# Third layer's gate weights by repeating transfers instead of a matmul, the shared expert first in each batch

## Chip, cores and metric

One core of a Trainium2 chip. The metric is device time in microseconds (us) of one execution of the whole kernel. Lower is better.

## What is computed

The reference is a stack of four layers on x of shape (4, 512, 128) in float32. Each layer has an attention-like block and a feed-forward block, each behind a layer norm and a gate tanh(g). The change touches the feed-forward block of the third layer (`L2_...` in the reference, `l == 2` in the kernel), a mixture of 32 small experts and one shared expert:

```
scores = sigmoid(X @ gate_w.T)
idx = top_k(scores + bias, 4)
w = scores[idx] / sum(scores[idx])
valid = position of the row in its expert's queue < 128
h_e = silu(X @ W1[e]) * (X @ W3[e])        # 64 hidden numbers for each of 32 experts
out = sum over the chosen, valid e of  w_e * (h_e @ W2[e])
out = out + (silu(X @ sw1.T) * (X @ sw3.T)) @ sw2.T
```

The kernel computes all 32 experts for all rows and multiplies the hidden numbers by the weight w_e, which is zero where a row did not choose the expert.

## The kernel before

The kernel is one program with hand-written instruction streams for five sequencers: `sync` (SP, issues transfers), `gpsimd` (POOL), `scalar` (ACT), `tensor` (PE) and `vector` (DVE). They meet at semaphores only (`wait_ge`, `then_inc`), and each engine takes its instructions in the written order, so a wait holds all that is written behind it.

**Units.** In the third layer's feed-forward block the work is cut into 4 batches of 512 rows (`b`) and 17 units in each (`c`). A routed unit holds a pair of experts, 2 x 64 hidden numbers on 128 partitions, for 512 rows; there are 16 (`ROUTED[2]`). The unit c = 16 is the shared expert. A unit goes through five steps:

1. `gu` on PE: two products for the gate (bank G) and two for the up projection (bank U), from the two parts `xt_hi` and `xt_lo` of the transposed input. For a routed unit a fifth matmul, called the pick here, multiplies the 0/1 matrix `pair_sel` by `comb_t`, the weights of all 32 experts turned and split into three bf16 parts. It spreads the two weight rows of this unit over 2 x 64 partitions of bank W.
2. `unit` on ACT: silu of G into the ring `hb` of four buffers (L887). `high` on ACT: copy of the bank W to one of three buffers `wsb` (L900).
3. `mult` on DVE: hb times U (L2303).
4. `low` on POOL: hb times wsb (L672); not for the shared expert.
5. `down` on PE: `wa_hi` times hb, summed over the 17 units in the bank ACC.

PE runs `gu` three units ahead of `down` (`AHEAD = 3`): at step c of the loop it does `gu` of unit c + 3, then `down` of unit c, then what else is written at this step. All matmuls go through a helper and carry L1172; the tile names tell them apart (`xt_hi,wa_hi`, `comb_t,pair_sel` the pick, `hb,wa_hi` the down).

**What lies between the units.** During batch b the next batch is prepared: layer norm (`moments`, `scale_rows`), transposition, logits on PE (`PE_LOGITS` = 5), the choice of experts in seven parts on DVE at the steps of `ROUTE_AT[2]`, the running count of rows in each expert on PE (`running`, step `PE_RUN` = 11), its use in `route_end` on DVE (`WEIGH_AT[2]` = 14), the turned weights on PE (`comb_in`, step `PE_COMB[2]` = 13) and their copy on ACT (`pre_comb`, `COMBT_AT[2]` = 16). In batches 0 and 1 the Fourier filter of the third layer's other block runs for batches 2 and 3 at the steps of `fft_steps`: moments, `split_halves` on DVE, `transform` on PE, `filter_products` on DVE, `inverse` on PE, `fft_update` on DVE. From unit 20 on, `chain` also puts the fourth layer's attention and routing in between. All of these share the one bank T: each use waits until the one before is read (`T_free`).

**Transfers.** SP issues transfers in one written order: the last of them before the fourth layer are `rows_of(2)` and `rows_of(3)` (L537, results of the second layer), and after `x_done` of the last Fourier update the fourth layer's weights (L589 to L592: three transfers of 16 experts' matrices, three of the shared expert's).

Of the kernel before, what the change touches and what calls it, by code (L numbers as in the profile page):

```python
# [14 lines left out]
F32 = mybir.dt.float32  # L15
# [8 lines left out]
TB = S // 128  # L24
# [188 lines left out]
def build(nc, a, out, s1, s3, y3, stages=8):  # L213
    with ExitStack() as ctx:
# [6 lines left out]
        def sem(name):  # L221
# [86 lines left out]
        d_x = [sem(f"d_x{b}") for b in range(B)]  # L308
        d_stage = [sem(f"d_stage{i}") for i in range(2)]
# [5 lines left out]
            um_done wcopy_done w_used zp_set ids_set sel3_done cum3_ps idx3_done cnt3_ps nb3_done incl3_ps  # L315
# [73 lines left out]
        wsb = nc.alloc_sbuf_tensor_at("wsb", [128, 3, 512], F32, offset=at["h_hi"])  # L389
        wpr = nc.alloc_sbuf_tensor_at("wpr", [128, E1, 4, 128], F32, offset=at["wa_lo"])[:, :, :, :]  # L390
# [33 lines left out]
        def slots(layer, c):  # L424

            if layer == 0:
                return (c, 16 + c, 32 + c) if c < 16 else (48, 49, 50)
            if layer == 2:
                return (c, 16 + c, 32 + c) if c < 16 else (48, 49, 50)
            return c, 20 + c, 40 + c  # L430
# [55 lines left out]
        ROUTE_AT = [(8, 9, 10, 11, 12, 13, 13), (16, 16, 16, 17, 18, 19, 20), (8, 8, 8, 9, 10, 11, 12), (8, 8, 8, 9, 10, 11, 12)]  # L486
        COUNT_AT = 10
        WEIGH_AT = [14, 21, 14, 13]
        COMBT_AT = [16, 24, 16, 15]
        PE_BACK, PE_XN, PE_LOGITS, PE_RUN = 0, 2, 5, 11  # L490
        PE_COMB = [13, 21, 13, 12]
# [4 lines left out]
        def fft_steps(l, b):  # L496


            if l == 2 and b < 2:
                return 2 + b, (4, 7, 8, 11, 10, 13)  # L500
# [5 lines left out]
        def _(sp):  # L506
# [80 lines left out]
            sp.wait_ge(q["x_done"], x_num(4, 3))  # L587
            for i, w in enumerate(("routed_w1", "routed_w2", "routed_w3")):
                sp.dma_start(pk3[:, :, F3 * i:F3 * i + F3], a["L3_ffn_" + w].rearrange("e d h -> d e h")).then_inc(d_wl, 16)  # L589
            sp.dma_start(hi_flat[:, 0:512], a["L3_ffn_shared_w1"][0]).then_inc(d_wl, 16)  # L590
            sp.dma_start(hi_flat[:, 512:1024], a["L3_ffn_shared_w2"][0]).then_inc(d_wl, 16)
            sp.dma_start(sw3, a["L3_ffn_shared_w3"][0].rearrange("(c h) d -> h c d", c=4)).then_inc(d_wl, 16)  # L592
# [29 lines left out]
        def _(pool):  # L622
# [1982 lines left out]
```

## Time and profile before

| what | value |
|---|---|
| median of 3 runs | 880.02 us (879.59 to 883.28) |
| the profiled execution | 879.37 us, of it the span of the profile 877.6 us |
| mean granted TensorE clock | 0.934 of full speed |
| PE busy in the span | 754.7 us (86%) |
| DVE, ACT, POOL busy | 560.9, 375.4, 390.2 us |
| third layer's feed-forward block | about 538 to 731 us of the span |

Busy PE time is modelled: a matmul is shown from its start to its end, and the next starts before that. The distance from start to start is the better price of one in a row of many.

### The profile page before, as it was taken

How to read it: one execution, taken by the hardware profiler on the slowest of the kernel's cores; microseconds unless marked ns; L12 is line 12 of the kernel's file. 1: busy time of each engine (PE TensorE's matmuls, PEld its weight loads, DVE VectorE, ACT ScalarE, POOL GpSimd, SP SyncE). 2: the span in 40 equal slices, each digit the busy share in tenths (PEclk: the TensorE clock that was granted, in tenths of full speed). 3: DMA queues.
4: the chain of work that ended last, by engine and by line, in shares of the span. 5: the costliest groups of instructions: out<-in, count | busy, mean ns of one | idle time of the engine just before them, and what ended most of it. 6: DMA issues, size and time to landing. Idle time of an engine off the chain costs nothing.

```text
span 877.6 us, 14107 instructions
## 1 busy us (share of the span) xinstructions
PE 754.7 (86%) x3936; PEld 536.6 (61%) x3936; DVE 560.9 (64%) x1813; ACT 375.4 (43%) x834; POOL 390.2 (44%) x381
## 2 busy tenths in 40 slices
PE   6999789999999878875997887999989887988885
PEld 3577656666767545665887885565555553645553
DVE  3377778878788278863533766978767644524554
ACT  0244244444445335524554434456455564213331
POOL 2000034545455435372764434555455663345661
PEclk8899989999999879955999998999999999899998
DMA  5023999800000311015677642000600000022325
GB/s 144 13 61 110 337 332 333 260 1 1 0 1 1 89 20 31 18 38 177 190 213 213 188 116 55 1 1 1 174 13 10 10 13 13 17 59 80 88 53 144
DMA packets 74396, 79.36 MB, mean 90 GB/s; under 512 B 17769, under 2 KB 61424, under 8 KB 74194
## 3 DMA queue, kind: packets, MB, share of 16 engines
q1 hardware_dynamic: 68112, 69.49, 27.4%
q0 software_dynamic: 5024, 8.54, 2.9%
q8 instruction: 35, 0.57, 0.3%
q10 hardware_dynamic: 1186, 0.43, 0.2%
q14 instruction: 39, 0.32, 0.1%
HBM read 40.48 MB, written 39.85 MB: 92 GB/s over the span
## 4 chain that ended last, share of the span: by engine, by line
PE 57%; DVE 23%; issue 7%; ACT 4%; POOL 3%; DMA 3%; SPq 1%; ACTq 0%; POOLq 0%; DVEq 0%
PE psum L1172 52%; DVE hb L2305 2%; DVE hb L2306 1%; POOL s L740 1%; DVE hb L2303 1%; DVE mr L1970 1%; DVE const L1926 1%; PE psum L1231 1%; POOL s L718 1%; PE psum L1621 1%; PE psum L1691 1%; DMA chosen<-in_mask_1x1xSxS_ik 1%; DVE l_lo L1886 1%; DVE wk L1927 1%; DMA l_hi<-y 1%
## 5 line engine op out<-in xcount | busy, mean ns | idle before, releaser
L677 POOL TENSOR_TENSOR h_lo<-hb,h_hi 128x512 fp32r<-128x512 f32 x68 | 87.8, 1294 | 119.7 <-ACT h_hi L905 119.6
L1172 PE MATMUL psum<-xt_hi,wa_hi 128*128 128x512 f32 x272 | 129.0, 474 | 13.1 <-DVE hb L2306 8.4
L745 POOL DMA_INDIRECT y<-xn x93 | 92.3, 993 | 77.7 <-DVE xn L2062 37.2
L887 ACT ACTIVATE hb<-psum 128x512 f32<-128x512 f32 x136 | 81.0, 595 | 81.5 <-PE psum L1172 81.3
L1172 PE MATMUL psum<-xt_lo,wa_hi 128*128 128x512 f32 x272 | 108.4, 399 | 0.0
L672 POOL TENSOR_TENSOR hb<-hb,wsb 128x512 f32<-128x512 f32 x64 | 82.1, 1283 | 56.2 <-DVE hb L2303 49.3
L1172 PEld LDWEIGHTS psum<-xt_hi,wa_hi 128*128 128x128 f32 x272 | 52.7, 194 | 36.0 <-DVE hb L2306 14.1
L2303 DVE TENSOR_TENSOR hb<-hb,psum 128x512 f32<-128x512 f32 x68 | 46.0, 684 | 39.9 <-ACT hb L887 29.4
L1172 PE MATMUL psum<-hb,wa_hi 128*128 128x512 f32 x136 | 70.9, 602 | 0.5 <-POOLq L674 0.5
L1172 PE MATMUL psum<-l_lo,l_hi 128*128 (+1 forms) x204 | 57.1, 380 | 10.9 <-issue 5.6
L1172 PEld LDWEIGHTS psum<-xt_lo,wa_hi 128*128 128x128 f32 x272 | 52.5, 193 | 16.1 <-issue 7.5
L648 POOL TENSOR_TENSOR rstd<-veps,neghalf 128x4 f32<-128x4 f32 x20 | 20.3, 1016 | 92.9 <-DVE veps L1864 92.1
L905 ACT ACTIVATE h_hi<-hb 128x512 fp32r<-128x512 f32 x68 | 42.7, 627 | 42.0 <-DVE hb L2306 41.4
L2305 DVE TENSOR_TENSOR hb<-hb,psum 128x512 f32<-128x512 f32 x64 | 43.7, 683 | 22.5 <-PE psum L1172 17.3
L1172 PE MATMUL psum<-comb_t,pair_sel 96*128 96x512 bf16 x128 | 50.8, 397 | 5.7 <-ACT wsb L900 5.0
L1172 PE MATMUL psum<-xt_hi,wa_lo 128*128 128x512 f32 x136 | 53.6, 394 | 0.0
L1172 PE MATMUL psum<-wpr,hb 128*128 x368 | 49.4, 278 | 0.3 <-issue 0.3
L1172 PEld LDWEIGHTS psum<-l_lo,l_hi 128*128 128x128 f32 x204 | 31.6, 192 | 27.5 <-issue 24.2
L1172 PEld LDWEIGHTS psum<-wpr,hb 128*128 128x128 f32 x368 | 45.8, 196 | 0.5 <-issue 0.5
L2306 DVE TENSOR_TENSOR hb<-hb,psum 128x512 f32<-128x512 f32 x64 | 44.0, 687 | 2.2
L718 POOL DMA_INDIRECT s<-l_hi,l_lo x32 | 31.3, 978 | 26.8 <-DVE l_hi L2200 14.5
L740 POOL DMA_INDIRECT s<-l_hi,l_lo x32 | 31.7, 992 | 25.4 <-DVE l_hi L2200 9.0
(353 smaller groups left out, 1714.6 us busy)
## 6 DMA issues: line engine op xcount, KB each, us to landing
s<-l_lo SPq DMA_DIRECT2D x20, 1386.0 KB, 16.8
l_hi<-in_pack SPq DMA_DIRECT2D x24, 322.0 KB, 3.3
l_lo<-in_pack SPq DMA_DIRECT2D x22, 322.0 KB, 3.7
xn<-s SPq DMA_DIRECT2D x93, 66.0 KB
stage<-in_pack SPq DMA_DIRECT2D x13, 256.0 KB, 2.6
y_in<-y SPq DMA_DIRECT2D x8, 256.0 KB, 4.0
l_hi<-y SPq DMA_DIRECT2D x8, 256.0 KB, 5.0
stage<-in_L_ffn_W SPq DMA_DIRECT2D x12, 128.0 KB, 2.3
```

What stands on the lines that cost most here:

```text
L648: pool.tensor_tensor(rstd[:, :], veps[:, :], neghalf[:, :], ALU.pow).then_inc(q["rstd_set"], 1)
L672: pool.tensor_tensor(hb[:, k % 4, :], hb[:, k % 4, :], wsb[:, w % 3, :], ALU.mult).then_inc(q["w_used"], 1)
L677: pool.tensor_tensor(h_lo[:, k % 3, :], hb[:, k % 4, :], h_hi[:, k % 3, :].bitcast(F32), ALU.subtract).then_inc(q["hlo_pool"], 1)
L718: pool.indirect_dma_start(s1, bass.IndirectOffsetOnAxis(idx3[:, n, i, k:k + 1], 0), xs3[i][:, TB * n + k, :], None).then_inc(d_scat1[n // ...
L740: pool.indirect_dma_start(s3, bass.IndirectOffsetOnAxis(idx3[:, n, i, k:k + 1], 0), xs3[i][:, TB * n + k, :], None).then_inc(d_scat, 16)
L745: pool.indirect_dma_start(y3, bass.IndirectOffsetOnAxis(xe3[:, j % XE, 128:129].bitcast(I32), 0), xe3[:, j % XE, 0:128], None, bounds_chec ...
L887: act.activation(hb[:, k % 4, :], G[k % 2][:, :], ACT.Silu).then_inc(q["sg_done"], 1)
L905: act.activation(h_hi[:, k % 3, :], hb[:, k % 4, :], ACT.Copy).then_inc(q["hhi_done"], 1)
L1172: return pe.matmul(o, l, r, start=start, stop=stop, skip_group_check=True)
L2303: dve.tensor_tensor(h, h, U[k % 2][:, :], ALU.mult).then_inc(q["um_done"], 1)
L2305: link(dve.tensor_tensor(h, h, U[k % 2][:, :], ALU.mult))
L2306: dve.tensor_tensor(h, h, W[k % 2][:, :], ALU.mult).then_inc(q["h_done"], 1)
```

## The change

- `comb_in` of the third layer turns the float32 weights (`wfin`, four transposes) instead of three bf16 parts. `route_end` on DVE ends with the multiplication that writes `wfin`; the four instructions that split it fall away for this layer.
- `pre_comb` on ACT copies the turned weights (32 x 512) to `wt2` and issues a transfer of them to a new table `wd` in device memory (4 x 32 x 512 float32).
- SP then loads, for each of the 64 routed units, two rows of `wd`, each repeated over 64 partitions, into one of the three buffers `wsb` (two transfers of 64 x 2 KB). It waits for the table of the batch, and from the fourth load on for POOL to be done with the buffer.
- The pick on PE and the copy `high` on ACT fall away for this layer. POOL's `low` waits for the transfer instead of the copy.
- The shared expert is unit c = 0 of each batch; the routed pairs are c = 1 to 16.
- The fourth layer's weights are loaded from within this sequence, behind the load for routed unit 36 (the fifth of batch 2), as `load_layer3()`.
- Steps move: route parts from (8, 8, 8, 9, 10, 11, 12) to (8, 8, 8, 8, 9, 9, 10), `PE_RUN` 11 to 8, `WEIGH_AT` 14 to 11, `PE_COMB` 13 to 10, `COMBT_AT` 16 to 13, the Fourier steps from (4, 7, 8, 11, 10, 13) to (6, 9, 12, 14, 14, 16).

```diff
+        d_wt, WT0 = d_wnat, 16 * 4
+        d_wb, WB0 = d_w1[0:3], [16 * len(range(i, NB1, WS)) for i in range(3)]
...
+        wt2 = nc.alloc_sbuf_tensor_at("wt2", [32, 512], F32, offset=at["comb_t"])
+        wfin = nc.alloc_sbuf_tensor_at("wfin", [128, TB, 32], F32, offset=at["chl"])
...
+            for b in range(B):
+                for c in range(ROUTED[2]):
+                    w = b * ROUTED[2] + c
+                    if c == 0:
+                        sp.wait_ge(d_wt, WT0 + 16 * (b + 1))
+                    if w >= 3:
+                        sp.wait_ge(q["w_used"], w - 2)
+                    for e in range(2):
+                        sp.dma_start(wsb[64 * e:64 * e + 64, w % 3, :],
+                                     wd[b, 2 * c + e:2 * c + e + 1, :].broadcast_to([64, S])).then_inc(d_wb[w % 3], 16)
+                    if w == 2 * ROUTED[2] + 4:
+                        load_layer3()
...
-                    if c >= ROUTED[2]:
+                    if c == 0:
                         pool.sem_inc(q["h_done"], 1)
                         return
-                    w = b * ROUTED[2] + c
-                    pool.wait_ge(q["wcopy_done"], w + 1)
+                    w = b * ROUTED[2] + c - 1
+                    pool.wait_ge(d_wb[w % 3], WB0[w % 3] + 32 * (w // 3 + 1))
...
+                if l == 2:
+                    if b:
+                        act.wait_ge(d_wt, WT0 + 16 * b)
+                    act.activation(wt2[:, :], T[0:32, :], ACT.Copy).then_inc(q["combt_done"], 1)
+                    act.wait_ge(q["combt_done"], fnum(l, b))
+                    act.dma_start(wd[b], wt2[:, :]).then_inc(d_wt, 16)
+                    return
...
-                    act.wait_ge(q["u_done"], UB[2] + k - CB[2] + 1)
-                    if w >= 3:
-                        act.wait_ge(q["w_used"], w - 2)
-                    if w == 0:
-                        act.wait_ge(q["down_done"], CB[2])
-                    act.activation(wsb[:, w % 3, :], W[0][:, :], ACT.Copy).then_inc(q["wcopy_done"], 1)
...
-                if l == 2 and k - CB[2] >= 1:
-                    pe.wait_ge(q["wcopy_done"], sum(1 for i in range(k - CB[2]) if i % NC[2] < ROUTED[2]))
...
-                    last = mm(W[0 if l == 2 else k % 2][:, :], pick, comb_t[0:3 * N_EXP[l], b % 2, :], True, True)
+                    last = mm(W[k % 2][:, :], pick, comb_t[0:3 * N_EXP[l], b % 2, :], True, True)
...
-                    link(dve.tensor_tensor(w_, w_, m_, ALU.mult))
+                    dve.tensor_tensor(wfin[:, :, :], w_, m_, ALU.mult).then_inc(q["comb_done"], 1)
+                    return
```

## Rows read from the trace of the kernel before

**Rows 1.** The page: the chain that ended last, by engine.

```profile
PE 57%; DVE 23%; issue 7%; ACT 4%; POOL 3%; DMA 3%; SPq 1%; ACTq 0%; POOLq 0%; DVEq 0%
```

**Rows 2.** Stretches: length, then PE, PEld, DVE, ACT, POOL busy, PEclk, DMA, GB/s.

```profile
545.00:580.00 35.00, 34.02 (x153) 20.99 (x152) 32.54 (x79) 17.13 (x31) 19.64 (x16) 1.00 0.00 1
...
590.00:618.00 28.00, 26.94 (x129) 17.16 (x128) 24.54 (x75) 16.54 (x30) 13.61 (x12) 1.00 0.00 1
```

**Rows 3.** The chain that ended last, by line, 545 to 727 us.

```profile
by line: PE psum L1172 56.9%; issue 6.8%; DVE hb L2303 5.5%; DVE wk L1909 2.1%; ACT hb L887 2.0%; ACT L887 1.8%; DVE mr L1970 1.5%; ACT wsb L900 1.5%; PE psum L1249 1.4%; DVE ch L2086 1.4%; DVE l_lo L1886 1.4%; DVE l_lo L2190 1.3%; DVE wk L
```

**Rows 4.** Timeline around a routed unit: start us, us, engine, line, operation.

```profile
562.14 0.39 PE L1172 MATMUL psum<-comb_t,pair_sel 96*128 96x512 bf16 x1
...
562.37 1.02 PE L1172 MATMUL psum<-hb,wa_hi 128*128 128x512 f32 x2
...
562.68 0.69 DVE L2303 TENSOR_TENSOR hb<-hb,psum 128x512 f32<-128x512 f32 x1
...
563.45 1.28 POOL L672 TENSOR_TENSOR hb<-hb,wsb 128x512 f32<-128x512 f32 x1 [0.95 <-DVE hb L2303]
...
564.15 0.39 PE L1172 MATMUL psum<-comb_t,pair_sel 96*128 96x512 bf16 x1
```

**Rows 5.** PE's waits, 545 to 727 us: us in total, times, longest.

```profile
PE psum L1172 <- ACT wsb L900: 5.0, 11, 0.7
...
PE psum L1172 <- DVEq L2347: 1.1, 1, 1.1
```

**Rows 6.** Timeline of the block's start.

```profile
536.49 0.29 DVE L2167 TENSOR_TENSOR chosen<-chosen 128x128 f32<-128x128 f32 x1
...
538.01 0.66 PE L1409 MATMUL psum<-ident_bf,chl 128*96 128x128 bf16 x4 [3.40 <-DVE chl L2171]
...
539.30 2.03 SPq L537 DMA_DIRECT2D y_in<-y  x4
...
545.40 1.02 PE L1172 MATMUL psum<-hb,wa_hi 128*128 128x512 f32 x2
```

**Rows 7.** Two stretches of that start, columns as in Rows 2.

```profile
538.00:540.00 2.00, 1.99 (x8) 1.56 (x8) 0.00 (x0) 1.27 (x2) 0.00 (x0) 0.50 0.01 0
...
544.00:545.00 1.00, 1.00 (x6) 0.77 (x5) 0.47 (x1) 0.90 (x3) 1.00 (x2) 1.00 0.38 107
```

**Rows 8.** Timeline of SP's queue: the fourth layer's weights, first and last issue.

```profile
621.89 6.25 SPq L589 DMA_DIRECT2D l_lo<-in_L_ffn_routed_w  x3
...
632.22 0.43 SPq L592 DMA_DIRECT2D l_hi<-in_L_ffn_shared_w  x1
```

**Rows 9.** Line 592, the last of these transfers: issue to landing.

```profile
DMA to landing us min/median/max: 5.7/5.7/5.7
```

**Rows 10.** DMA issues: KB each, median us from issue to landing.

```profile
y_in<-y SPq DMA_DIRECT2D x8, 256.0 KB, 4.0
...
stage<-in_L_ffn_W SPq DMA_DIRECT2D x12, 128.0 KB, 2.3
```

**Rows 11.** A stretch of the fourth layer's loading, columns as in Rows 2.

```profile
626.00:628.00 2.00, 1.90 (x11) 1.06 (x10) 0.66 (x1) 1.76 (x4) 1.28 (x1) 1.00 1.07 295
```

**Rows 12.** Timeline, batch 2: POOL at c = 2 and c = 6, PE's down of c = 6.

```profile
637.62 1.28 POOL L672 TENSOR_TENSOR hb<-hb,wsb 128x512 f32<-128x512 f32 x1 [1.48 <-DVE hb L2303]
...
651.71 1.29 POOL L672 TENSOR_TENSOR hb<-hb,wsb 128x512 f32<-128x512 f32 x1
...
656.22 1.02 PE L1172 MATMUL psum<-hb,wa_hi 128*128 128x512 f32 x2
```

**Rows 13.** Timeline of DVE in batch 0: scaling for the filter, and routing scores.

```profile
556.55 3.19 DVE L1872 TENSOR_SCALAR wk<-x,mv,rstd 128x128 f32<-128x128 f32 x4
...
561.31 1.34 DVE L2086 TENSOR_TENSOR ch<-rt,small 128x128 f32<-128x128 f32 x1
```

**Rows 14.** Timeline of the block's last units: PE's down, POOL's multiplication.

```profile
725.42 1.12 PE L1172 MATMUL psum<-hb,wa_hi 128*128 128x512 f32 x2 [0.48 <-POOLq L674]
...
725.58 1.27 POOL L672 TENSOR_TENSOR hb<-hb,wsb 128x512 f32<-128x512 f32 x1 [0.27 <-POOL hb L672]
```

More of the change, by code:

```diff
@@ L210, in link, with build @@
         self.eng.wait_ge(self.sem, self.n)
-def build(nc, a, out, s1, s3, y3, stages=8):
+def build(nc, a, out, s1, s3, y3, wd, stages=8):
     with ExitStack() as ctx:
@@ L427, in slots @@
                 return (c, 16 + c, 32 + c) if c < 16 else (48, 49, 50)
-            if layer == 2:
-                return (c, 16 + c, 32 + c) if c < 16 else (48, 49, 50)
-            return c, 20 + c, 40 + c
+            return (c - 1, 15 + c, 31 + c) if c else (48, 49, 50)
         block = ctx.enter_context(nc.Block())
@@ L484, in build @@
         NORM_AT, OUT_AT, XN_AT, ADD_AT, XHI_AT, XLO_AT, SCORE_AT = 0, 2, 3, 3, 5, 6, 8
-        ROUTE_AT = [(8, 9, 10, 11, 12, 13, 13), (16, 16, 16, 17, 18, 19, 20), (8, 8, 8, 9, 10, 11, 12), (8, 8, 8, 9, 10, 11, 12)]
+        ROUTE_AT = [(8, 9, 10, 11, 12, 13, 13), (16, 16, 16, 17, 18, 19, 20), (8, 8, 8, 8, 9, 9, 10), (8, 8, 8, 9, 10, 11, 12)]
         COUNT_AT = 10
[L488 to L491, printed above, removed]
+        WEIGH_AT = [14, 21, 11, 13]
+        COMBT_AT = [16, 24, 13, 15]
+        PE_BACK, PE_XN, PE_LOGITS, PE_RUN = 0, 2, 5, 8
+        PE_COMB = [13, 21, 10, 12]
         NORM2_AT, XN2_AT = 4, 7
@@ L586, in _, with load_layer3 @@
             rows_of(3)
[L587 to L592, printed above, removed]
+            def load_layer3():
+                sp.wait_ge(q["x_done"], x_num(4, 3))
+                for i, w in enumerate(("routed_w1", "routed_w2", "routed_w3")):
+                    sp.dma_start(pk3[:, :, F3 * i:F3 * i + F3], a["L3_ffn_" + w].rearrange("e d h -> d e h")).then_inc(d_wl, 16)
+                sp.dma_start(hi_flat[:, 0:512], a["L3_ffn_shared_w1"][0]).then_inc(d_wl, 16)
+                sp.dma_start(hi_flat[:, 512:1024], a["L3_ffn_shared_w2"][0]).then_inc(d_wl, 16)
+                sp.dma_start(sw3, a["L3_ffn_shared_w3"][0].rearrange("(c h) d -> h c d", c=4)).then_inc(d_wl, 16)
+            for b in range(B):
[10 more added lines that the diff above has]
+                        load_layer3()
             sp.wait_ge(q["tabi_done"], 3)
@@ L1139, in _ @@
                             k = b * NC[l] + c
-                            if l == 2:
-                                high(l, b, c)
-                            elif k >= 1:
+                            if l != 2 and k >= 1:
                                 pb, pc = divmod(k - 1, NC[l])
@@ L1407, in comb_in @@
                 use_t()
-                for k in range(TB):
+                for k in range(TB if l == 2 else 0):
+                    last = pe.transpose(T[0:32, 128 * k:128 * k + 128], wfin[:, k, :], ident)
+                for k in range(0 if l == 2 else TB):
                     last = pe.transpose(T[:, :].bitcast(BF16)[0:rows, 128 * k:128 * k + 128], chl[:, k, 0:rows], ident_bf[:, :])
@@ L1435, in gu @@
                 last = product(U[k % 2][:, :], us)
-                if l == 2 and k - CB[2] >= 1:
-                    pe.wait_ge(q["wcopy_done"], sum(1 for i in range(k - CB[2]) if i % NC[2] < ROUTED[2]))
-                if c == 0:
+                if l == 0 and c == 0:
                     pe.wait_ge(q["combt_done"], fnum(l, b))
-                if c < ROUTED[l]:
-                    if N_EXP[l] == 32:
-                        pick = pair_sel[:, 2 * c:2 * c + 2, :].rearrange("p e i -> p (e i)")
-                    else:
-                        pick = sel16[:, c:c + 1].broadcast_to([48, 128])
-                    last = mm(W[0 if l == 2 else k % 2][:, :], pick, comb_t[0:3 * N_EXP[l], b % 2, :], True, True)
+                if l == 0 and c < ROUTED[l]:
+                    pick = pair_sel[:, 2 * c:2 * c + 2, :].rearrange("p e i -> p (e i)")
+                    last = mm(W[k % 2][:, :], pick, comb_t[0:3 * N_EXP[l], b % 2, :], True, True)
                 last.then_inc(q["u_done"], 1)
@@ L2601 @@
     y3 = nc.dram_tensor("y3", (2 * B * S, D), F32, kind="Internal").ap()
-    build(nc, a, out, s1, s3, y3, STAGES)
+    wd = nc.dram_tensor("wd", (B, 32, S), F32, kind="Internal").ap()
+    build(nc, a, out, s1, s3, y3, wd, STAGES)
     r = run_bass_kernel_spmd(nc, [arrays], core_ids=[0])
```

9 lines of the change are left out of this document (2 added, 7 removed).

## The prediction

> **What bounds the kernel now.** I read the page's chain first: of the whole span PE holds 57% of the chain that ended last, DVE 23% [rows 1]. Then the same chain over the block that the change touches: PE's matmuls 56.9%, the rest split over many DVE and ACT lines, and 1.5% for the ACT copy that the change removes [rows 3]. So PE sets the pace for something under two thirds of the block, and for the rest PE stands or would soon stand behind DVE. The busy time by stretch says where: from 545 to 580 us PE is busy 34.0 and DVE 32.5 of 35 us, from 590 to 618 us 26.9 and 24.5 of 28 [rows 2]. PE has hardly a gap, but DVE is close behind it; what PE saves there soon meets DVE. Last, the timeline of one unit: two picks in neighbouring units start at 562.14 and 564.15, so a routed unit costs PE 2.01 us, and the pick takes 562.14 to 562.37 of it, 0.23 us [rows 4].
>
> **What the picks give.** There are 64 picks. Four or five of them lie in the start (below); 59 x 0.23 = 13.6 us of PE time are left. All of it comes off the time only if PE is the path throughout. I take 0.6 of it, the share of the chain over the block that is PE's (56.9% and a little for other PE lines [rows 3]): 8.1 us. Ends: 5 us if DVE closes up early, 13.6 us if not at all.
>
> **What the ACT copies give.** PE waited 11 times, 5.0 us in all, for the copy to free the bank W [rows 5]; that wait is gone. The copy's share of the chain is 1.5% of 182 us = 2.7 us [rows 3]. I take 2.7; ends 0 and 5.0. The copies' other time on ACT was beside other work.
>
> **What DVE saves.** From the multiplication at 536.49 to the start of PE's transposes at 538.01 lie 1.52 us, of them about 0.35 for the multiplication; the split costs 1.15 us [rows 6]. Once per batch: the first belongs to the start. Of the other three, 3.4 us, a third is on the path: 1.0 us; ends 0 and 3.4. The four transposes in float32 instead of bf16 I cost at nothing; there are three such places outside the start, and even at twice their 0.66 us [rows 6] they would be under 2 us, a third of it on the path.
>
> **The start.** PE waited 3.4 us for the weights, started at 538.01 and reached its first down at 545.40 [rows 6]. Without the split it starts 1.15 us earlier. Its clock is granted at half (1.2 GHz) at 538 to 540 and is full (2.4 GHz) at 544 to 545 [rows 7]; at the half clock a pick costs twice 0.23, so the first five picks are worth some 1.7 us. But now a chain of transfers stands before POOL's first multiplication. SP issues four transfers of `rows_of` until 541.33 [rows 6], which run until 544.4 (0.38 of the last microsecond [rows 7]); the rows for the first routed unit are written behind them. The table itself is ready before: transposes and copy end near 538.2, and a small transfer takes 2.3 us [rows 10]. The first rows therefore land near 544.4 + 0.4 + 1.0 = 545.8, POOL ends at 547.1 [its 1.28 in rows 4], and PE's down of c = 1 starts at 547.2. Before it stood at 545.40 + 2.02 = 547.4. Of 2.9 us saved 0.2 to 0.4 arrive: I take 0.4. Ends: 2.9, and a loss of 2.
>
> **One unit's transfers, steady.** Two issues of about 0.4 us (as line 592 [rows 8]), then 2.3 us for 128 KB [rows 10] and about 0.4 us for the second 128 KB at the 295 GB/s of the fourth layer's loading [rows 11]: 3.5 us. Three buffers go round in 3.5 + 1.3 (POOL) + 0.2 = 5.0 us, 1.7 us a unit, below the 2.01 - 0.23 = 1.78 us that PE needs. So they are hidden, narrowly; at the mean pace of the block, (727 - 545) / 68 = 2.7 us before and some 2.6 after, amply. Since (6.3 + 1.5) / 3 = 2.6, up to 6.3 us for a pair costs nothing on average. The nearest rows for the other end are the 256 KB with 4.0 us [rows 10], so up to 5.5 us. At a batch's first unit the table is ready in time: PE turns it at step 10, eight units (20 us) before its first row is multiplied.
>
> **The fourth layer's weights.** This is the queue that matters. Before, nobody waited for them. Now rows are written before and behind them in SP's order. SP issues them from 621.89 to 632.65 [rows 8], and the last lands at 632.22 + 5.7 = 637.9 [rows 8, 9]: 16.0 us, with the transfer engines full [rows 11]. SP reaches them when POOL is done with routed unit 33, which is c = 2 of batch 2. The rows of unit 37 (c = 6) can land only 0.9 (the issue of unit 36) + 16.0 + 1.4 (its own data and that of unit 36) = 18.3 us after that. Before, POOL ended c = 2 at 638.90 and began c = 6 at 651.71, 12.8 us [rows 12]; with a faster PE some 12. POOL stands 6.3 us. PE is less hit: its down of c = 6 began at 656.22, 3.2 us after POOL's end at 653.00 [rows 12]. So PE stands 3.1 us, and falls to half clock for a time, as after the wait of 3.4 us [rows 6, 7]; at half clock for about 3 us it loses 1.4 more. I take +4.5 us; ends 0 (DVE is late there anyway, and works ahead meanwhile) and 11 (no slack, and a load that is stretched by the rows between).
>
> Here the Trainium skill has a rule, in DMA: Bandwidth & Descriptors, section Queues, rings and completion order: each transfer engine takes the descriptors of one issuing engine's ring in order. By it the rows of unit 37 wait for the whole load. Rows 8 and 9 agree as far as they go, with the last issued landing 16 us after the first issue. If the order did not hold, this term would be near 0 and the sum 4.5 us lower.
>
> **The last unit.** Before, the shared expert closed the block, and needed no POOL. Now the last down waits for POOL's 1.27 us behind the unit before it [rows 14]: +1.4 us; ends 1 and 2.
>
> **The moved steps.** Before, `running` stood at step 11 of PE behind the Fourier update of DVE's step 13 in bank T; PE waited 1.1 us for that once [rows 5]. That goes: -1.1. But DVE's step 9 now holds marking, choice and, in batches 0 and 1, the scaling for the filter (3.19 us) and the split; its step 8 the scores (1.34 us) [rows 13] and the top values. Together the steps 8 and 9 have some 10 us of DVE work against 2 units of PE (4 us), and PE's `comb_in` at step 10 waits for DVE's step 11. A lead of up to three units pays most of it. I take +1.5 us for the two batches; ends 0 and 5.
>
> **Sum.** -8.1 - 2.7 - 1.0 - 0.4 + 4.5 + 1.4 - 1.1 + 1.5 = -5.9 us. The profiled execution took 879.37, so 873.5; the median stands 0.65 higher, so 874.
>
> **Rivals.**
>
> *DVE closes up (no change).* For it: DVE at 93% from 545 to 580 us [rows 2]. The picks then give 5 us, the copies 1, and the terms of cost stay: -5 - 1 - 1 - 0.4 + 4.5 + 1.4 - 1.1 + 2.5 = 0: 880. Against it: from 618 us on DVE has gaps. The change would then do what it says, off the path.
>
> *PE's whole saving arrives.* -13.6 - 5.0 - 2 - 0.4 + 2 + 1.4 - 1.1 + 0 = -18.7: 861. It needs DVE to keep ahead everywhere; against it the near-equal loads of rows 2.
>
> *The fourth layer's load is worse (within or above).* The term at its end of 11, the rest as forecast: 880.5.
>
> *Repeated rows are read slowly (slower).* All 64 copies of a row come from the same 2 KB of memory, which no row of the trace shows. It decides from 6.3 us for a pair on; POOL waits in each unit. At 7 us a unit takes (7 + 1.5) / 3 = 2.83 us instead of 2.6, over 64 units +15 us on the forecast: 889. At 8 us it is +36: 910. Against it: rates of 295 GB/s for 512-byte pieces from separate places [rows 11], and 2 KB pieces here. The Trainium skill, same page, section Latency and other measured facts, tells of loads whose rows lie a large power of two apart and run at half rate (103 of 207 GB/s), with reads falling on the same part of memory as its guess. By it the 256 KB of a pair would take 2.5 us instead of 0.9 and the pair 5.1, still under the point from which it decides; no row here shows it.
>
> **Chances.** Forecast (867 to 876): 0.42. PE's whole saving (below 867): 0.10. DVE closes up: 0.20. Load worse: 0.12. Slow rows: 0.16. Faster by over 0.5% (below 875.6; 0.5% is about what this measurement can tell from no change): 0.50. Within: 0.26. Slower (above 884.4): 0.24. The range 862 to 888 leaves out half of the second case and the worse half of the last one; the forecast's own range is 867 to 876.
>
> **What would show it.** Right: the block some 6 us shorter; one stand of POOL of about 6 us at routed unit 37 with transfer engines full, and PE at half clock behind it; no PE wait for a copy; the first POOL multiplication near 545.8; the last down behind POOL. The landing of a pair at 3 to 4 us shows the rate; 7 or more, with POOL idle before each unit, shows the slow rows. A longer PE wait before the turned weights of batches 1 and 2 shows DVE's crowded step 9. I am wrong if PE's matmuls keep their spacing of 2.0 us because DVE holds them, or if the stand at unit 37 is absent or beyond 10 us.

## The result and the profile after

| | before | after |
|---|---|---|
| median of 4 runs | 879.81 us (878.27 to 883.28) | 896.46 us (894.50 to 897.05) |
| span of the profiled execution | 877.6 us | 894.4 us |
| mean granted clock | 0.934 | 0.916 |
| PE, DVE, ACT, POOL busy | 754.7, 560.9, 375.4, 390.2 us | 754.8, 543.6, 340.4, 390.1 us |

The ratio is 1.0178 [1.0151, 1.0205]: the change makes the kernel 1.8% slower, some 16 us, where I had forecast 0.7% faster. (Before was run again beside each set of experiments, with medians from 879.8 to 882.7 us; a ratio compares within its set and leaves disturbed executions out. A difference of two medians carries up to 3 us of that drift, so where both are given the ratio is the better figure. Where a ratio is turned into us below, it is taken times 881 us.)

The page's groups first, to see that the change does what it says. Columns: line, engine, tiles, shape, count, busy us, mean ns, then idle time before and what ended most of it; then the issues with KB each and us to landing.

```profile
L690 POOL TENSOR_TENSOR hb<-hb,wsb 128x512 f32<-128x512 f32 x64 | 82.1, 1282 | 55.4 <-DVE hb L2313 37.1
...
L2313 DVE TENSOR_TENSOR hb<-hb,psum 128x512 f32<-128x512 f32 x68 | 45.7, 684 | 36.7 <-ACT hb L912 31.1
...
wsb<-wd SPq DMA_DIRECT2D x128, 128.0 KB, 2.8
```

There are 128 row loads, no pick and no copy, and ACT lost 35 us of work. A transfer of repeated rows lands in 2.8 us, so a pair with its two issues of 0.6 takes 3.4 to 4.0 us, near the 3.5 assumed. Yet PE is busy as long as before over the span: 13.6 us of picks are gone, and the other matmuls took that much longer in sum. In the block itself (from the turned weights to the last batch's end) PE is busy 173.2 us instead of 177.0, and idle 32.0 us instead of 15.5. The reason is in the waits, and the clock behind them. PE's waits, 536 to 760 us (us in total, times, longest):

```profile
PE psum L1184 <- POOLq L692: 12.1, 3, 7.4
PE psum L1184 <- DVE hb L2313: 11.4, 11, 2.0
PE psum L1280 <- DVE wk L1918: 7.2, 3, 5.3
PE psum L1421 <- DVE wfin L2176: 2.2, 1, 2.2
```

The same before, 536 to 731 us, besides [rows 5]:

```profile
PE psum L1172 <- DVE hb L2303: 4.2, 4, 1.8
PE psum L1268 <- DVE wk L1909: 3.7, 3, 1.6
PE psum L1172 <- POOLq L674: 0.5, 1, 0.5
```

Line 1184 is PE's matmul helper, 692 POOL's hand-over of a routed unit, 1280 the transposition of the fourth layer's attention probabilities, 1421 `comb_in`. The 5.0 us of waiting for ACT's copies [rows 5] are gone; in their place are 12.1 us for POOL where there were 0.5, and 18.6 us for DVE (lines 2313 and 1918) where there were 7.9. The longest sit at three places.

**The fourth layer's weights, batch 2.** SP's queue, then POOL and PE (start us, us, engine, line; idle before in brackets):

```profile
651.83 7.86 SPq L594 DMA_DIRECT2D l_lo<-in_L_ffn_routed_w  x3
659.74 3.31 SPq L595 DMA_DIRECT2D l_hi<-in_L_ffn_shared_w  x1
663.10 0.43 SPq L596 DMA_DIRECT2D l_hi<-in_L_ffn_shared_w  x1
663.57 0.46 SPq L597 DMA_DIRECT2D l_hi<-in_L_ffn_shared_w  x1
664.08 4.45 SPq L607 DMA_DIRECT2D wsb<-wd  x6
```

```profile
659.82 1.28 POOL L690 TENSOR_TENSOR hb<-hb,wsb 128x512 f32<-128x512 f32 x1 [2.13 <-DVE hb L2313]
662.01 1.06 POOL L758 DMA_INDIRECT s<-l_hi,l_lo  x1 [0.91 <-POOL hb L690]
671.48 1.25 POOL L690 TENSOR_TENSOR hb<-hb,wsb 128x512 f32<-128x512 f32 x1 [8.41 <-issue]
```

```profile
665.04 0.40 PE L1184 MATMUL psum<-xt_lo,wa_hi 128*128 128x512 f32 x1
672.84 2.08 PE L1184 MATMUL psum<-hb,wa_hi 128*128 128x512 f32 x2 [7.40 <-POOLq L692]
```

Stretches around it (length; PE, PEld, DVE, ACT, POOL busy; clock, DMA share, GB/s):

```profile
660.00:668.00 8.00, 5.44 (x26) 3.63 (x25) 3.26 (x12) 3.13 (x5) 2.16 (x2) 1.00 1.03 297
668.00:670.00 2.00, 0.00 (x0) 0.00 (x0) 0.00 (x0) 0.00 (x0) 0.00 (x0) 0.89 0.96 220
670.00:682.00 12.00, 9.16 (x21) 5.83 (x22) 4.03 (x17) 2.25 (x4) 6.79 (x6) 0.50 0.27 88
```

From the first issue to POOL's multiplication of routed unit 37 lie 19.6 us; I had forecast 17.4. The timeline says "issue" where POOL waits for this transfer; the transfer engines at 1.03 and 0.96 show what it was. PE stands 7.4 us, until 672.84. The clock falls to half, 1.2 GHz, during the stand, between 669 and 670 us, and all that PE does from 672.84 to 682 it does at half: the down that takes 1.02 us [rows 12] takes 2.08. Of these 9.16 us of matmuls half would have sufficed, so the clock costs another 4.6 us. Here the Trainium skill's rule (DMA: Bandwidth & Descriptors, section Queues, rings and completion order: descriptors of one ring are taken in order) agrees with the trace: the load's last piece, issued at 663.57, landed 7.1 us later, at 670.7, and the six row transfers behind it took 4.5 to 6.7 us to land instead of 2.8. But that is the smaller part. SP needed from 651.83 to 664.08, 12.2 us, to issue the load, and before that it could not issue a row at all.

**Batch 1, the routing and the fourth layer's attention.** DVE, then PE:

```profile
615.21 0.75 DVE L2142 TENSOR_SCALAR chosen<-mr 128x128 f32<-128x128 f32 x1
...
616.46 1.12 DVE L1881 TENSOR_SCALAR wk<-x,mv,rstd 128x128 f32<-128x128 f32 x4
617.61 0.42 DVE L2324 TENSOR_TENSOR wk<-wk 128x256 f32<-128x256 f32 x1
...
619.20 1.13 DVE L2160 TENSOR_SCALAR wsum<-wsum 128x4 f32<-128x4 f32 x1
...
621.43 0.29 DVE L1918 TENSOR_TENSOR wk<-wk,const 128x128 f32<-128x128 f32 x1
```

```profile
621.78 1.03 PE L1280 MATMUL psum<-const,wk 128*32 128x128 f32 x4 [5.25 <-DVE wk L1918]
```

Marking, Fourier scale, split and weights all stand ahead of the normalisation of the attention (L1918), for which PE waits 5.25 us. Before, the same wait in this batch was 0.6 us.

**The start.** PE, then POOL:

```profile
542.47 0.61 PE L1421 MATMUL psum<-const,wfin 128*32 128x128 f32 x4 [2.23 <-DVE wfin L2176]
...
549.39 1.02 PE L1184 MATMUL psum<-hb,wa_hi 128*128 128x512 f32 x2
...
554.15 2.07 PE L1184 MATMUL psum<-hb,wa_hi 128*128 128x512 f32 x2 [2.81 <-POOLq L692]
```

```profile
552.58 1.46 POOL L690 TENSOR_TENSOR hb<-hb,wsb 128x512 f32<-128x512 f32 x1 [3.28 <-DMA wsb<-wd]
```

The first multiplication comes 10.1 us after the turned weights; PE stands 2.8 us, and its matmuls take twice as long, at a granted clock of 0.50 from 554 to 560 us. From the turned weights to the down of c = 1 pass 11.7 us (542.47 to 554.15); before, 9.4 (538.01 to 547.42).

**Where in the block.** From each trace I take the start of the turned weights' transposes and the four starts of the `out_back` transposes (each at step 0 of the next batch, the last at the block's end), and get four stretches that can be compared. Behind the label stands the ratio to before of all its runs. The last column is the time in the block at the half clock: twice the sum of (1 - PEclk) times length over stretches of about 5 us:

| kernel | ratio | block begins | batch 0 | 1 | 2 | 3 | block | at half clock |
|---|---|---|---|---|---|---|---|---|
| before | | 538.0 | 50.0 | 50.1 | 51.1 | 41.3 | 192.5 | 9 |
| after | 1.0178 | 542.5 | 54.9 | 51.1 | 57.2 | 42.1 | 205.3 | 34 |
| l3_spread | 1.0070 | 538.2 | 55.3 | 51.0 | 49.1 | 40.9 | 196.3 | 18 |
| old_steps | 1.0033 | 537.6 | 49.6 | 47.6 | 56.2 | 42.1 | 195.6 | 25 |
| spread_old | 0.9994 | 540.4 | 49.9 | 47.6 | 48.2 | 40.6 | 186.2 | 12 |
| dummy_picks | 1.0060 | 543.8 | 51.0 | 49.3 | 50.0 | 44.2 | 194.7 | 12 |
| picks_shared_first | 1.0003 | 542.5 | 49.9 | 49.0 | 48.7 | 43.2 | 190.8 | 4 |
| picks_new_order | 1.0136 | 545.9 | 54.2 | 55.2 | 51.1 | 42.6 | 203.1 | 13 |
| fft_wide | 1.0020 | 540.0 | 52.9 | 50.7 | 48.3 | 42.3 | 194.2 | 24 |
| transform_late | 1.0050 | 539.5 | 53.0 | 52.0 | 50.2 | 41.6 | 196.7 | 26 |

The block begins anywhere from 534.9 to 546.6 us in the 20 traces of this study, 541.3 on average in the four kernels' traces with picks and the old copies and 540.6 in the sixteen without, so the 4.5 us by which it begins later here are hardly the change's. The scatter goes with the clock ahead of the block: 78 us at the half clock where the block begins earliest, 90 in before, 113 where it begins latest. The 12.8 us in the block are the change's; the ratio says 15.7 (13.3 to 18.1), and the traces don't place the difference. A block's length scatters too: in the traces of spread_old, first_rows_early and few_rows_old (all below), with the same routing and Fourier steps, it is 186.2, 191.5 and 191.9 us.

### The profile page after: what moved, and what is told of

Its sections match the earlier page's. It is cut to its first block, busy times and chain, and to the rows that moved or that the text cites. A ratio compares the mean times of both kernels' runs of the same rounds, so it can differ in the third digit from the quotient of the medians.

```text
span 894.4 us, 13966 instructions
## 1 busy us (share of the span) xinstructions
PE 754.8 (84%) x3872; PEld 543.9 (61%) x3872; DVE 543.6 (61%) x1797; ACT 340.4 (38%) x770; POOL 390.1 (44%) x381
## 4 chain that ended last, share of the span: by engine, by line
PE 56%; DVE 23%; issue 8%; POOL 4%; DMA 3%; ACT 3%; SPq 1%; ACTq 0%; POOLq 0%; DVEq 0%
PE psum L1184 51%; DVE hb L2315 2%; DVE hb L2313 2%; DVE hb L2316 1%; POOL s L758 1%; DVE mr L1979 1%; PE psum L1243 1%; DVE const L1935 1%; POOL s L736 1%; PE psum L1630 1%; PE psum L1700 1%; DMA chosen<-in_mask_1x1xSxS_ik 1%; DVE wk L1936 1%; DMA l_hi<-y 1%; POOL hb L690 1%
## 5 line engine op out<-in xcount | busy, mean ns | idle before, releaser
L1184 PE MATMUL psum<-xt_hi,wa_hi 128*128 128x512 f32 x272 | 131.7, 484 | 20.2 <-DVE hb L2313 11.4
L1184 PE MATMUL psum<-hb,wa_hi 128*128 128x512 f32 x136 | 76.0, 642 | 12.1 <-POOLq L692 12.1
L1184 PE MATMUL psum<-l_lo,l_hi 128*128 (+1 forms) x204 | 57.3, 380 | 10.8 <-issue 5.6
L919 ACT ACTIVATE h_hi<-hb 128x512 fp32r<-128x512 f32 x68 | 42.6, 627 | 41.9 <-DVE hb L2316 41.4
L1184 PE MATMUL psum<-wpr,hb 128*128 x368 | 49.9, 280 | 0.3 <-issue 0.3
L986 ACT ACTIVATE hb<-psum,l_hi 128x128 f32<-128x128 f32 x96 | 27.4, 368 | 32.0 <-PE psum L1184 32.0
```

The source lines that it names most:

```text
L919: act.activation(h_hi[:, k % 3, :], hb[:, k % 4, :], ACT.Copy).then_inc(q["hhi_done"], 1)
L986: last = act.activation(hb[:, j % 4, 128 * c:128 * c + 128], G[j % 2][:, 128 * c:128 * c + 128], ACT.Gelu_apprx_tanh, bias=w1s[j % WS][:, ...
L1184: return pe.matmul(o, l, r, start=start, stop=stop, skip_group_check=True)
```

## The experiments

**l3_spread: the load in small pieces.**

```diff
-                    if w == 2 * ROUTED[2] + 4:
-                        load_layer3()
+                    if 0 <= w - (2 * ROUTED[2] + 4) < 15:
+                        load_layer3(w - (2 * ROUTED[2] + 4))
...
+                if j < 12:
+                    i, g = divmod(j, 4)
+                    w = ("routed_w1", "routed_w2", "routed_w3")[i]
+                    sp.dma_start(pk3[:, 4 * g:4 * g + 4, F3 * i:F3 * i + F3],
+                                 a["L3_ffn_" + w][4 * g:4 * g + 4].rearrange("e d h -> d e h")).then_inc(d_wl, 16)
```

> The changed kernel, but the fourth layer's weights in 15 transfers of 256 KB, one behind each of the row loads 36 to 50, instead of all behind load 36. Theory A (the stand of PE at routed unit 37, 7.4 us in the trace of the changed kernel, and the half clock behind it until 683 us cost 11 to 13 us): 883 to 886 us, no PE wait over 2 us in batch 2, clock full there. Rival B (the stand only uses time that DVE would have taken anyway, or the row loads slow PE's loop everywhere): under 4 us gained, 892 to 897.

888.77 us, ratio 1.0070 [1.0037, 1.0104]. The stand of 7.4 us is gone and batch 2 falls from 57.2 to 49.1 us. The load in one piece cost 7.7 us by the medians, 9.5 by the ratios, less than theory A and more than rival B.

**old_steps: the steps of before, the rest as changed.**

```diff
-        WEIGH_AT = [14, 21, 11, 13]
-        COMBT_AT = [16, 24, 13, 15]
-        PE_BACK, PE_XN, PE_LOGITS, PE_RUN = 0, 2, 5, 8
-        PE_COMB = [13, 21, 10, 12]
+        WEIGH_AT = [14, 21, 14, 13]
+        COMBT_AT = [16, 24, 16, 15]
+        PE_BACK, PE_XN, PE_LOGITS, PE_RUN = 0, 2, 5, 11
+        PE_COMB = [13, 21, 13, 12]
...
-                return 2 + b, (6, 9, 12, 14, 14, 16)
+                return 2 + b, (4, 7, 8, 11, 10, 13)
```

> The changed kernel with the steps of before: route parts, running count, turned weights and Fourier steps at their old places; rows by transfer and shared expert first stay. Theory A (DVE's crowded step 9 of batch 1 holds the fourth layer's attention and so PE for 5.3 us, plus some 2 us of half clock): 6 to 8 us faster than the changed kernel, 888 to 891, and no wait of that size before the turned probabilities. Rival C (the moved steps are neutral, what is won at one place is lost at another, such as the old coupling of the running count to the Fourier update): within 2 us of 896.5.

886.84 us, ratio 1.0033 [0.9995, 1.0071]: 9.6 us by the medians, 12.8 by the ratios, more than even theory A. Batches 0 and 1 fall by 5.3 and 3.5 us. This was the bigger surprise: I had priced these steps at 1.5 - 1.1 = +0.4 us.

**picks_new_order: before, with the shared expert first and the new steps; picks and copies stay.**

```diff
+            return (c - 1, 15 + c, 31 + c) if c else (48, 49, 50)
...
-                return 2 + b, (4, 7, 8, 11, 10, 13)
+                return 2 + b, (6, 9, 12, 14, 14, 16)
```

> The kernel before (picks on PE, copies on ACT), but the shared expert first in each batch and the moved steps of the change. Theory A (the moved steps cost 6 to 8 us, the last routed unit 1.5): 887 to 890. Rival C (order and steps are neutral; all the loss is in the transfers): 880 to 882.

894.38 us, ratio 1.0136 [1.0104, 1.0169]. Without a single row load, order and steps cost 12 us, again above both forecasts.

**before_again: the kernel before, unchanged.**

> The kernel before, unchanged, profiled once more. In the changed kernel the block started 4.5 us later than in the first profile of before, though nothing ahead of it was changed. If that is chance from run to run, this profile lies anywhere from 538 to 543 us at the first turned weights; if it belongs to the changed program, this one is again at 538 us.

880.41 us. Its block took 192.5 us, as in the first trace, and batches 0 and 1 50.1 each. It begins at 538.9 us, with 89 us at the half clock ahead of it. That looked like the program's own beginning; the other traces with picks, at 542.5 and 545.9, say that it is not.

**spread_old: l3_spread and old_steps together.**

> The changed kernel with both repairs: the fourth layer's weights in fifteen transfers of 256 KB, one behind each of the row loads 36 to 50, and the steps of the kernel before. Theory (two separate costs, the load and the crowded steps): the two savings of 7.7 and 9.6 us add, 896.5 - 17.3 = 879, about equal to before or a little faster, with no PE wait of more than 4 us for POOL. Rival (the same time is saved twice, because the DVE that stands behind is the bound after either repair): 884 to 887. Rival (faster than both kernels, since the picks and copies are gone): 872 to 876.

881.73 us, ratio 0.9994 [0.9966, 1.0021]. Both savings are there; together they give back the whole 1.8%, though not their sum (9.5 + 12.8). In its trace the block is 6.3 us shorter than before, begins 2.4 us later, and is followed by 149.5 us to the end of the span instead of 147.1; behind the block 23 us are at the half clock, 17 before. The whole is 1.5 us shorter in this trace, and level with before over all executions.

**picks_shared_first: before with the shared expert first, old steps.**

> The kernel before, with its picks and copies and its steps, but the shared expert first in each batch. Theory (the moved steps cost the time, the order almost nothing): 880 to 882. Rival (the order itself costs: POOL stands once per batch and works one unit later at the end, and PE's last down waits for it): 884 to 890, most of the 12 us of picks_new_order.

882.43 us, ratio 1.0003 [0.9968, 1.0039]. The order costs nothing. So the 12 us of picks_new_order are the steps'.

**few_rows: after, with 61 of 64 pairs never loaded** (POOL multiplies by old rows).

```diff
-                    for e in range(2):
+                    for e in range(2 if w < 3 else 0):
```

> The changed kernel, but only the first three pairs of rows are loaded, and POOL multiplies by those old buffers from then on; the loads of the other 61 routed units are left out, all steps and the load of the fourth layer's weights stay. Theory (the rows cost only where they queue behind the fourth layer's weights): 888 to 890, as l3_spread, and no wait of POOL for a transfer behind the first unit. Rival (the 8 MB of row loads slow other things too, ports or memory): 880 or less. Rival (the rows cost nothing, PE would stand anyway): 895.

889.46 us, ratio 1.0086 [1.0052, 1.0119], as l3_spread. The row loads (128 of 128 KB, so 16 MB and not the 8 that I had written) cost what they wait behind the fourth layer's weights, and nothing more that can be seen (1.0086 against l3_spread's 1.0070).

**few_rows_old: the same on spread_old.**

> spread_old, but only the first three pairs of rows are loaded and POOL multiplies by those old buffers from then on; the loads of the other 61 routed units are left out. It is the change with its transfers free of cost. Theory (PE's saved time is given back at DVE, not at the transfers): 880 to 882, as spread_old. Rival (the row loads still cost POOL or PE some us): 875 to 877.

882.19 us, ratio 0.9971 [0.9929, 1.0013], not to be told from spread_old (881.73 us, 0.9994). By the medians the transfers are free; the two intervals together leave anything from 6 us of cost to 2 us of gain open.

**dummy_picks: the picks put back, unread, on spread_old.**

```diff
+                if l == 2 and c:
+                    last = mm(W[0][:, :], pair_sel[:, 0:2, :].rearrange("p e i -> p (e i)"), hi.bitcast(BF16)[0:96, 0:512], True, True)
```

> spread_old with a matmul of the pick's shape (96x128 weights, 96x512 bf16 moving) put back for each of the 64 routed units, its result never read; everything else as spread_old. It prices the picks alone. Theory (PE's picks lie in time in which PE would wait for DVE, or in which the filled engine keeps its clock): 881 to 883, no change against spread_old. Rival (the picks are worth my 8 us and something else in the change costs as much): 889 to 891.

885.01 us, ratio 1.0060 [1.0037, 1.0084], 3.3 us over spread_old by the medians, 5.8 by the ratios, 8.5 in the blocks of the two traces. It lies between the two theories. The picks are worth something, 3 to 8 us, near my 8.1 at best. And with them in place the rest of the change costs 5.3 us (3.3 to 7.4), which I had forecast at a small gain.

**first_rows_early: three pairs of rows ahead of the second layer's results.**

```diff
-            rows_of(2)
-            rows_of(3)
...
+                    if w == 2:
+                        rows_of(2)
+                        rows_of(3)
...
-                            if l == 2 and b == 0 and c in (2, 3):
-                                combine1(c)
+                            if l == 2 and b == 0 and c in (4, 5):
+                                combine1(c - 2)
```

> spread_old with the loads of the first three pairs of rows ahead of the two loads of the second layer's results, whose adding on DVE moves from steps 2 and 3 to 4 and 5 of batch 0. Theory (the first multiplication on POOL waits behind those 1 MB loads, and PE falls to half clock for it): the first POOL multiplication comes 3 to 4 us earlier, 878 to 879 against 881.7. Rival (DVE holds batch 0 anyway): 881 to 882.

877.90 us, ratio 0.9974 [0.9951, 0.9997]. POOL's first multiplication:

```profile
541.71 1.26 POOL L698 TENSOR_TENSOR hb<-hb,wsb 128x512 f32<-128x512 f32 x1
```

That is 6.8 us after the turned weights (534.88) instead of 10.1 to 10.9, and batch 0 takes 48.5 us instead of 49.9. The gain over spread_old, 1.8 us by the ratios, is within both intervals.

**fft_old and route_old: half of the moved steps each.** fft_old is after with only the Fourier steps old; route_old is after with only the routing's.

> The changed kernel with only the Fourier steps of the kernel before (4, 7, 8, 11, 10, 13); routing stays at its new steps. Theory (DVE's step 9 is crowded because the Fourier scale and split were put beside the routing marks): PE's waits for the attention's probabilities shrink and most of the 9.6 us of old_steps comes back, 888 to 890. Rival (the early running count and turned weights at PE's steps 8 and 10 are what holds PE): no gain, 895 to 897. Rival (the shared bank T is taken in a worse order when only one half moves): slower than 897.

> The changed kernel with only the routing steps of the kernel before (parts, running count, weights, turned weights, copy); the Fourier steps stay at the new ones. The other half, the old Fourier steps alone, gave 899.7 us. Theory (the routing parts packed into DVE's steps 8 to 11 are the whole cost of the moved steps): 886 to 888, as with both moved back. Rival (both halves must move together, since all share the bank T): 893 or more.

fft_old 899.7 us, 1.0212 [1.0179, 1.0246]; route_old 891.66 us, 1.0105 [1.0059, 1.0150]. Neither half gives back what both do (1.0033): the old routing steps alone bring 6.4 us, between my two forecasts, and the old Fourier steps alone bring nothing. By its time fft_old is what the third possibility said, slower than 897, but its interval overlaps that of the changed kernel (1.0178 [1.0151, 1.0205]), so that it is worse is not shown. The two sets depend on each other; the runs don't show by which wait.

**parts_early: only the seven routing parts on DVE early, on spread_old.**

> spread_old with only the seven routing parts on DVE at their new steps (8, 8, 8, 8, 9, 9, 10); running count, weights, turned weights, copy and Fourier steps stay old. Theory (the parts packed together hold DVE's multiplications of two or three units, and PE stands for them): 2 to 5 us over spread_old, 884 to 887. Rival (the parts are only handed over in another order, the cost is that running count and turned weights take the bank T and PE's time early): 881 to 883.

882.17 us, ratio 1.0021 [0.9990, 1.0053]. Packing the parts is no cost that the runs can show, though its trace has batch 1 at 51.0 us with a wait of 3.8 us for the attention's normalisation (1.8 in spread_old). A cost of up to 2 us stays possible.

**new_steps_b2: the new routing steps in batch 2 alone, which has no Fourier filter.**

> spread_old with all new routing steps (parts, running count 8, weights 11, turned weights 10, copy 13), but in batch 2 only, which has no Fourier filter beside it. Theory of the prediction's term (the cost comes where the Fourier scale and split stand beside the routing, batches 0 and 1): 881 to 882. Rival (the routing's own packing costs in each batch): a third of the 12 us, 885 to 886.

877.76 us, ratio 0.9962 [0.9930, 0.9994], below both forecasts. No cost there. What the routing's steps cost, they cost in batches 0 and 1, beside the Fourier filter.

**fft_wide and transform_late: the distance between PE and DVE.** In l3_spread DVE, for once, waits for PE (DVE, then PE, batch 0):

```profile
580.87 0.42 DVE L2342 TENSOR_TENSOR wk<-l_lo,psum 128x256 f32<-128x256 f32 x1 [3.05 <-PE psum L1191]
...
587.33 0.88 DVE L2359 SCALAR_TENSOR_TENSOR x<-psum,tg,x 128x256 f32<-128x256 f32 x2 [2.88 <-PE psum L1191]
```

```profile
578.83 1.95 PE L1191 MATMUL psum<-wk,const 128*128 128x128 f32 x16
...
585.35 1.95 PE L1191 MATMUL psum<-wk,const 128*128 128x128 f32 x16
```

These are the Fourier filter's products behind `transform`, and its update behind `inverse`. Before, they stood three steps behind PE's (8 to 11, 10 to 13), with the change two (12 to 14, 14 to 16). PE runs `gu` three units ahead, so in step c of DVE, three steps on from PE's step c - 3, the products of `gu` are there already. A result that PE makes in step c - 2 may not be, and then DVE waits for it. First the edit of l3_spread to fft_wide, then that of spread_old to transform_late:

```diff
-                return 2 + b, (6, 9, 12, 14, 14, 16)
+                return 2 + b, (6, 9, 11, 14, 13, 16)
...
-                return 2 + b, (4, 7, 8, 11, 10, 13)
+                return 2 + b, (4, 7, 9, 11, 10, 13)
```

> l3_spread (all new steps) with the Fourier steps (6, 9, 11, 14, 13, 16) instead of (6, 9, 12, 14, 14, 16): PE transforms and inverts one step earlier, so that DVE's products and update stand three steps behind, as in the kernel before. Theory (DVE is held by PE because it comes two steps behind): its two waits of 3 us per batch go, the first two batches take 51 and 48 us, and the time falls from 888 to 882 to 884. Rival (the routing packed into DVE's steps 8 to 11 is the cause, the Fourier distance is not): 887 to 890.

> spread_old (all old steps) with PE's transform at step 9 instead of 8, so that DVE's products stand two steps behind it. Theory (the distance of two steps costs DVE's lead): DVE waits some 2 to 3 us for PE ahead of the products, and the time rises by 2 to 4 us over spread_old, 884 to 886. Rival (no cost by itself): 881 to 883.

fft_wide 883.38 us, 1.0020 [0.9990, 1.0051], 4.4 us under l3_spread by the ratios. transform_late 886.77 us, 1.0050 [1.0023, 1.0078], 4.9 us over spread_old. DVE's waits for PE in l3_spread, in fft_wide, in spread_old and in transform_late, 538 to 650 us:

```profile
DVE x L2359 <- PE psum L1191: 6.2, 2, 3.3
DVE wk L2342 <- PE psum L1191: 6.1, 2, 3.1
```

```profile
DVE x L2359 <- PE psum L1191: 2.6, 2, 1.7
DVE wk L2342 <- PE psum L1191: 2.5, 2, 1.3
```

```profile
DVE wk L2342 <- PE psum L1191: 1.7, 2, 1.3
```

```profile
DVE wk L2342 <- PE psum L1191: 6.2, 2, 3.5
```

One step of distance, given or taken, moves the waits by 4 to 7 us and the time by 4 to 5 (each plus or minus 3 to 4), both ways. Moving the step also moves PE's use of the bank T; no run tells that apart from the distance, though DVE's waits are for the result itself. The forecast for fft_wide was right in the time and half right in the stretches: batch 0 fell only from 55.3 to 52.9, batch 1 hardly (PE's wait for the attention stays, 5.2 us).

**shared_last: first_rows_early, with the shared expert last in batches 1 to 3.**

> first_rows_early with the shared expert first in batch 0 only and last in batches 1 to 3. Theory (with the shared expert first PE's last down waits for POOL's last multiplication, 1.4 us): 1 to 2 us under first_rows_early, 876 to 877. Rival (the end is hidden by other work): equal, 878.

880.01 us, ratio 0.9987 [0.9964, 1.0010]. No gain, where I had forecast 1 to 2 us: a last down that needs no POOL is worth nothing that can be measured.

**all_repairs: shared_last with new_steps_b2's steps.**

> The best of all: the change with the fourth layer's weights spread over fifteen loads, the steps of the kernel before in batches 0 and 1 and the new routing steps in batch 2, the first three pairs of rows ahead of the second layer's results, the shared expert first in batch 0 and last in the others. Theory (the repairs add, and the picks are worth what I forecast): 874 to 878, under before by 0.4 to 0.9%. Rival (what is won in this block is lost to what follows): 880 to 882.

880.57 us, ratio 0.9991 [0.9966, 1.0015]. A miss. The small gains of first_rows_early and new_steps_b2 don't add up; nothing here beats the kernel before by more than their 0.3 to 0.4%, of which the intervals just exclude zero.

## Why the prediction was wrong

**What the moved steps cost** is the step of the prediction that failed most: +1.5 for "crowded DVE step 9" and -1.1 for the freed bank T, together +0.4 us. Measured: 11.7 us (picks_new_order against picks_shared_first), 12.8 (after against old_steps), 6.7 where the load no longer stands in the way (l3_spread against spread_old). I had looked for what DVE does in a step, and named the right place for one part of it: the marks, the Fourier scale and the split in one run of DVE. But I let `comb_in` wait for it, and paid it from a lead of three units. In the trace the one that waits is the fourth layer's attention, queued on DVE behind all this; what that wait costs by itself stays open, for parts_early has 3.8 us of it and no slower time. And the lead itself had been cut: two steps between `transform` and the products, and between `inverse` and the update, where before there were three. The numbers (8 to 11, 12 to 14) stood in the diff. fft_wide and transform_late show that this is 4 to 5 us; of the rest the stretches tell only that it lies almost all in batches 0 and 1, and the halves that it depends on both sets of steps. Which wait carries it stays open. The -1.1 came true: the wait for bank T is in no line of the trace after.

**The fourth layer's load** was the right place at half its size: +4.5 forecast, 7.7 to 9.5 measured (the ratios leave 6 to 13). From its first issue to POOL's multiplication passed 19.6 us where I had 17.4 (18.3 less the 0.9 of issue before it). POOL was to stand 6.3 and stood 10.4 (661.10 to 671.48, with one indirect transfer of 1.06 in it): SP reached the load 9.3 us before POOL ended the last unit that had its rows, against 11 assumed. PE was 3 us less late than POOL, as I had it, hence 7.4 instead of 3.1. And PE's work at the half clock behind the stand lasted more than 9 us, not 3: I had sized its stretch by the length of the stand, which [rows 6] and [rows 7] never supported. That is 4.6 us against 1.4. My upper end of 11 holds the measured value. One reading of mine was wrong besides: without the order in the ring the term would not have been near 0. SP's issuing alone held the next rows back for 12.2 us, and their waiting behind the load in the transfer engines adds up to 3.9 (6.7 us to land instead of 2.8). The rows of [rows 8] had both in them: 10.8 of the 16.0 us were issuing.

**The picks**: 8.1 forecast, 3.3 to 5.8 measured in time (the ratios leave 3 to 9), 8.5 in the blocks of two single traces, of which 3.6 are in batch 3 and within its scatter. The size was near the forecast's lower end of 5. Where the rest of 13.6 goes, the clock tells in part. From the block's begin to the end of the span PE's clock is at half for 20 to 28 us in the four traces with the old steps and with the picks or a matmul in their place (before, before_again, picks_shared_first, dummy_picks), and for 27 to 47 us in four with the old steps and none (spread_old, few_rows_old, first_rows_early, shared_last). The means are 25 and 38 us; the 13 us between them are worth up to 6.5, by my estimate from these traces. That the missing picks are the cause, no run shows.

**The repeated rows** were the largest risk of a clear slowdown that I gave, 0.16, and did not come: a transfer lands in 2.8 us, and few_rows shows no cost of the rows beyond their wait behind the load. The Trainium skill's half rate for rows a large power of two apart (same page, section Latency and other measured facts) is not seen here: from 562 to 564 us, where SP issues nothing but rows, 126 GB/s take 0.35 of the transfer engines, and [rows 11] has 295 GB/s at 1.07. But these rows repeat one address, which is another case than the section's.

**The start**: -0.4 forecast. From turned weights to POOL's first multiplication 10.1 us passed, where my numbers had 8.9 (545.8 less 536.9), and a second stretch at the half clock came with PE's stand. The down of c = 1 comes 2.3 us later behind the turned weights than before, of which the split that is gone gives back 1.15; 6 us of work at the half clock are worth 3 more. So the trace has the start at about +4. In spread_old batch 0 takes 49.9 us, as before, though sixteen picks of 0.23 are gone from it; the start can hold all of them.

**The last unit**: +1.4 forecast. PE waits 1.9 us for POOL there, but shared_last doesn't gain by it.

**The copies and the split**: -2.7 and -1.0 were not tried alone. dummy_picks says that the change without its picks' saving, its steps and its load in one piece costs +5.3 us, where these terms, the start and the last unit had summed to -2.7. Of these 8 us the start holds some 2 by first_rows_early's ratio, some 4 by the trace. The float32 transposes, which I had at nothing, are not it: four take 1.03 us at the half clock (540.38 in spread_old), four in bf16 0.66. The rest stays open; nothing here shows which part it is.

**Where the range failed**: I had taken the upper ends for separate cases, and several happened together. Even so, all of them in one sum (-5 for the picks, 0 for copies and DVE, +2 for the start, 11, 2, -1.1 and 5) give +13.9, 894 us, and 896.5 were measured. What no end held were the steps: 5 at most, 7 to 13 measured.

## What to carry to other kernels

When steps in a hand-written order are moved, write down for each pair of producer and consumer on two engines how many steps lie between, before and after, and hold it against the lead by which one engine runs ahead: one step less cost 0.5% here, with the work unchanged. A bulk load written into a queue that now carries short deadlines belongs in pieces between them; the same bytes, spread, cost nothing that shows. Count the time that the queue's owner needs to issue it (12.2 us here), not only the transfer. And a stand of PE must be priced with the half clock behind it: 4.6 us behind the stand of 7.4, and at the start some 3 us behind one of 2.8, as much as the stand itself.

## What the hardware showed that I had not expected

- A row of 2 KB repeated over 64 partitions loads nearly as fast as other data: 128 KB land in 2.8 us (median of 128, at most 6.7), other transfers of 128 KB in the same trace in 2.4. An issue takes 0.6 us.
- Within a stand of 7.4 us the granted clock fell to 0.50 (1.2 GHz), and it stayed there for the first 9.16 us in which PE then worked without a gap. In the start it was 0.50 from 554 to 560 us with PE busy 5.85 of 6 us, behind a stand of 2.8 us.
- Saved PE work hardly lowered PE's busy time: 13.6 us of picks less, and 177.0 us busy in the block before, 173.2 after, with 9 and 34 us at the half clock.
- Nearly the same code reaches this block between 534.9 and 546.6 us in 20 traces, with 78 to 113 us at the half clock ahead of it. One trace can't tell a few us in what precedes the edit.
